# A graph layer on one core: in-place exponentials in two halves, and a third pair buffer in PSUM

## The reference, cut to what matters

```
w_m = (efeat @ W_msg + b_msg).reshape(E, in_f, -1)
w_a = (efeat @ W_attn + b_attn).reshape(E, in_f, -1)
h_src = feat[src][:, :, None]
e1 = w_m * h_src
e2 = w_a * h_src
ex = jnp.exp(e2 - seg_max[dst])
denom = jax.ops.segment_sum(ex, dst, num_segments=N)
ft = jax.ops.segment_sum(e1 * (ex / denom[dst]), dst, num_segments=N)   # then .sum(axis=1)
```

## Time and profile before

| | |
|---|---|
| time, median of 3 runs | 3181.63 us (3181.13 to 3204.2) |
| the profiled execution | 3216.98 us, span 3215.1 us |
| PE busy | 2134.1 us (66%) |
| DVE busy | 1858.7 us (58%) |
| ACT busy | 1255.2 us (39%) |
| POOL busy | 1686.0 us (52%) |
| TensorE clock granted, mean | 0.83 |

### The profile page before, as it was taken

One profiled execution on the slowest core, in us unless ns is written; L12 is line 12 of the kernel. 1 busy time (PEld: TensorE's weight loads), 2 busy tenths in 40 slices (PEclk: granted clock), 3 DMA queues, 4 the chain that ended last, 5 costly groups with the idle time before them and its releaser, 6 DMA issues. The chain is left out here.

```text
span 3215.1 us, 21756 instructions
## 1 busy us (share of the span) xinstructions
PE 2134.1 (66%) x6682; PEld 953.8 (30%) x6682; DVE 1858.7 (58%) x2902; ACT 1255.2 (39%) x1228; POOL 1686.0 (52%) x1845
## 2 busy tenths in 40 slices
PE   2336678667787566766565558687777786667487
PEld 1212233223333222322222223233333332223233
DVE  6235466556665545655454456465667665666386
ACT  3113344334443334433333335353435444343354
POOL 6666555555564554444454444556565664536614
PEclk8657888878898787888887779888899998878799
DMA  6100000000000000000000000000000001001000
GB/s 210 15 14 10 11 10 10 10 9 9 9 14 9 9 9 8 8 12 8 8 9 7 8 7 12 9 9 11 8 12 11 9 12 22 11 7 16 8 1 3
DMA packets 60073, 47.60 MB, mean 15 GB/s; under 512 B 28366, under 2 KB 55439, under 8 KB 59436
## 3 DMA queue, kind: packets, MB, share of 16 engines
q0 software_dynamic: 57632, 29.73, 7.2%
q1 hardware_dynamic: 2316, 16.38, 1.4%
HBM read 44.00 MB, written 1.90 MB: 14 GB/s over the span
## 5 line engine op out<-in xcount | busy, mean ns | idle before, releaser
L652 POOL DMA_INDIRECT AR<-in_xt,AR x1607 | 1538.7, 958 | 751.3 <-issue 494.1
L1128 PE MATMUL PX<-AR,CS 128*128 128x512 f32 x3246 | 1660.3, 640 | 13.5 <-ACT AR L894 8.5
L1472 DVE CUSTOM_DVE_ANT_1 AR<-PW,AR 128x1024 f32<-128x1024 f32 x815 | 978.6, 1221 | 1172.2 <-remote 924.1
L1108 PE MATMUL PW<-WS,LT 100*128 100x512 bf16 x1630 | 551.7, 425 | 976.2 <-DVE AR L1472 755.0
L1128 PEld LDWEIGHTS PX<-AR,CS 128*128 128x128 f32 x3246 | 668.9, 207 | 633.6 <-issue 516.3
L888 ACT ACTIVATE LT<-PTB 100x1024 bf16<-100x1024 bf16 (+1 forms) x221 | 211.3, 956 | 1437.3 <-remote 1017.1
L1485 DVE TENSOR_TENSOR AR<-AR,PX 128x1024 f32<-128x1024 f32 (+1 forms) x442 | 501.2, 1134 | 113.8 <-ACT PX L944 87.1
L1108 PEld LDWEIGHTS PW<-WS,LT 100*128 100x128 bf16 x1630 | 140.0, 102 | 1398.0 <-DVE AR L1472 811.6
L946 ACT ACTIVATE AR<-AR 128x2048 f32<-128x2048 f32 (+1 forms) x221 | 413.0, 1869 | 7.2
L950 ACT ACTIVATE PX<-AR 128x1024 f32<-128x1024 f32 (+1 forms) x221 | 212.3, 961 | 330.7 <-DVE AR L1485 263.0
L657 POOL DMA_INDIRECT AR<-in_es,E0I x48 | 45.4, 946 | 556.2 <-issue 271.9
(11 more groups left out here) (192 smaller groups left out, 517.8 us busy)
## 6 DMA issues: line engine op xcount, KB each, us to landing
AR<-in_xt,AR POOLq DMA_INDIRECT x1607
AR<-in_eat SPq DMA_DIRECT2D x3, 3128.0 KB
AR<-in_eat SPq DMA_DIRECT2D x1, 3120.0 KB
y_d<-AR SPq DMA_DIRECT2D x1, 784.0 KB
AR<-y_d SPq DMA_DIRECT2D x1, 784.0 KB
AR<-in_es,E0I POOLq DMA_INDIRECT x48
y_d<-AR POOLq DMA_INDIRECT x36
CS<-in_cst SPq DMA_DIRECT2D x1, 442.0 KB, 5.3
```

The lines of the kernel that those rows point to most:

```text
L652: g.indirect_dma_start(feat(h, j - j0, j - j0 + 1), None, xt, bass.IndirectOffsetOnAxis(ap=node, axis=0)).then_inc(hg_sem(h), 16)
L1108: i = pe.matmul(PAIRS[s % 2][:, j, :], LT[:, g % 3, lo:lo + 128], WS[:, :], start=True, stop=True)
L1128: i = pe.matmul(PDR, IDN, x, start=(a == 0 and j == 0), stop=(g == LAST[k] and j == n - 1))
L1472: v.tensor_tensor_reduce(em(g, j, j + 2).rearrange("p (x c) -> p x c", c=32), w, hb, 1.0, LOW, ALU.mult, ALU.max, accum_out=MXC[:, k % 2, ...
```

## The change

The two PSUM banks `EXP` become a third pair buffer. Pair s now uses buffer s % 3 and waits for `v_mult` of pair s-3, and PE's W run three pairs ahead instead of two. ACT does two exponentials per group, each of one half and in place; the copy and the waits for `v_gm` are gone. `gm` reads both the messages and the exponentials from SBUF.

```diff
-        PAIRS = [PW[:, 0:2, :], PW[:, 2:4, :]]
-        EXP = PX[:, 0:2, :].rearrange("p b e -> p (b e)")
+        PAIRS = [PW[:, 0:2, :], PW[:, 2:4, :], PX[:, 0:2, :]]
...
                         x, w, shift = weights(c)
                         a.wait_ge(S["v_M"], GRP[c][0] + 1)
-                        if c >= 1:
-                            a.wait_ge(S["v_gm"], 2 * c)
-                        a.activation(half(w), x[:, 0:w, :], ACT.Exp, bias=shift).then_inc(S["a_x"], 1)
-                        a.wait_ge(S["a_x"], 2 * c + 1)
-                        a.activation(x, x, ACT.Exp, bias=shift).then_inc(S["a_exp"], 1)
-                    if c is not None:
-                        a.wait_ge(S["a_exp"], c + 1)
-                        a.wait_ge(S["v_gm"], 2 * c + 1)
-                        a.activation(half(w), x[:, w:2 * w, :], ACT.Copy).then_inc(S["a_x"], 1)
+                        for y in range(2):
+                            z = x[:, w * y:w * y + w, :]
+                            a.activation(z, z, ACT.Exp, bias=shift).then_inc(S["a_x"], 1)
...
-                    if s >= 2:
-                        pe.wait_ge(S["v_mult"], s - 1)
+                    if s >= 3:
+                        pe.wait_ge(S["v_mult"], s - 2)
...
-                        i = pe.matmul(PAIRS[s % 2][:, j, :], LT[:, g % 3, lo:lo + 128], WS[:, :], start=True, stop=True)
+                        i = pe.matmul(PAIRS[s % 3][:, j, :], LT[:, g % 3, lo:lo + 128], WS[:, :], start=True, stop=True)
...
-                            pe.wait_ge(S["a_exp"], g + 1)
+                            pe.wait_ge(S["a_x"], 2 * g + 2)
...
+                W(0, 2)
...
-                    ahead = [(p, x) for x in range(2, GRP[p][2] // 2)] if p is not None else []
-                    ahead += [(nx, 0), (nx, 1)] if nx is not None else []
+                    ahead = [(p, x) for x in range(3, GRP[p][2] // 2)] if p is not None else []
+                    ahead += [(nx, 0), (nx, 1), (nx, 2)] if nx is not None else []
...
-                    w = PAIRS[s % 2].rearrange("p j (i c) -> p (j i) c", c=32)
+                    w = PAIRS[s % 3].rearrange("p j (i c) -> p (j i) c", c=32)
...
-                    y = em(g).rearrange("p (x a o) -> p x a o", a=2, o=16)[:, w * h:w * h + w, 1, :]
-                    v.tensor_tensor(y, y, EXP[:, 0:16 * w].rearrange("p (x o) -> p x o", o=16), ALU.mult).then_inc(S["v_gm"], 1)
+                    y = em(g).rearrange("p (x a o) -> p x a o", a=2, o=16)[:, w * h:w * h + w, :, :]
+                    v.tensor_tensor(y[:, :, 1, :], y[:, :, 1, :], y[:, :, 0, :], ALU.mult).then_inc(S["v_gm"], 1)
```

More of the change, by code:

```diff
@@ L902, in weights @@
                     return em(g).rearrange("p (x a o) -> p x a o", a=2, o=16)[:, :, 0, :], 8 * n, CM[:, 1, k:k + 1]
-                def half(w):
-                    return EXP[:, 0:16 * w].rearrange("p (x o) -> p x o", o=16)
                 def first(k):
@@ L1489, in pairs @@
                     keep = KEPT(half)
-                    v.wait_ge(S["a_exp"], g + 1)
+                    v.wait_ge(S["a_x"], 2 * g + 2)
                     v.wait_ge(S["v_gm"], 2 * g + 2)
```

## The result

The changed kernel took 2890.86 us in the median of four runs (2833.12 to 2950.91), the kernel before 3183.88 us (3181.13 to 3204.2): a ratio of 0.8936, 95% interval 0.883 to 0.9041. The ratio goes by the two shortest runs of the changed kernel. The prediction, 3128 us in a range from 3050 to 3260, had the sign right and missed the time by 237 us, outside its range.

The account below looks back on a forecast made before the run. No one engine bound it: a bin's period was POOL's run of gathers, some 4 us, and a stretch with PE and DVE nearly full. -125 + 75 - 3 = -53 us on 3181.6 gave 3128 us, range 3050 to 3260.

Parts of the forecast that it names:

- the slow stretch: Within POOL's run of gathers in each bin: PE, DVE and ACT nearly stop, 40.5 and 21.7 us, PE's completions arriving late.
- gathers that follow each other less closely let PE's completions through sooner: Rival for the slow stretch: 2 us x 48 gained on top of the forecast, 3032 us; better outcomes together had 0.10.
- The cost on POOL: Weights multiply with two SBUF inputs lengthens gathers in POOL's long runs: 0.45 us on each of 168, +75 us.
- My own rival: POOL's gather runs lengthen more than the buffer saves: 0.8 us per multiply, 134 us, time 3256 us; chance 0.20.
- The gain in PE and DVE: Third pair buffer lets PE and DVE use idle time and adds lead: 2.6 us per bin, -125 us.
- The credit for one more pair at each slow stretch: With a third buffer PE does one more W and two `gsum` slots before it stops: 2.15 us per bin.
- ACT's relief: Two in-place half exponentials take about 2.0 us per large group off ACT; worth nothing on its own.
- the multiply keeps its duration: DVE's weights multiply with both inputs in SBUF: 1.23 us against 1.22 at 1024 columns, counted zero.
- My stop sign: The forecast is wrong if busy time of POOL's gathers, L652, grows by over 150 us.
- The harder form of the rival: DVE's multiply also waits for a gather to end: 0.36 us on average, 60 us more, 3316 us; chance 0.04.

Follow-up runs that it names:

- late case: First comparison, unedited kernels: before 3183.88 us, changed 2890.86 us; many of PE's semaphore increments come late, up to 53 us after the last recorded end.
- prompt case: Every run since, on six chips, PE's increments within 0.02 us: unedited kernel before 2242 to 2246 us, changed kernel 2510.68 us, ratio 1.1203.
- the operand and its wait: Kernel before with the weights multiply's second input taken from SBUF instead of PSUM, and the wait for in-place exponentials: 2484.02 us, ratio 1.1073.
- the 16 of the wait: Kernel before with only the added wait for the in-place exponentials, operand still in PSUM: 2260.58 us, ratio 1.0073.
- POOL relieved: Every second gather of bins 2 to 47 left out, timing only: kernel before 2160.06 us, changed 2140.13 us, changed with two pair buffers 2160.78 us.

## Why the prediction was wrong

**The step that failed is the first one, the slow stretch: "I don't know the mechanism; I take it as the trace shows it."** From there on it stood as a constant of the kernel, POOL's runs plus 4 us. It was neither of the kernel nor constant. The same program without it takes 2242 us, 942 less; since no edit is between the two, it belongs to the chip or to its condition at that time, which the record can't tell apart. And in the late case itself the changed kernel escaped it for hundreds of us at a time: DVE's idle time before its multiplies fell by 301 us, the time by 293. Nor does every run of gathers without a pause bring it on, as I had taken it: in the stretches of 220 and 328 us POOL issues one after the other, each of them longer (1158 and 1166 ns in the mean against 947), and PE's increments are prompt. I had the rival "gathers that follow each other less closely let PE's completions through sooner" and gave it, with another, 0.10 and 3032 us. Its arithmetic, 2 us a bin, allowed a shorter slow stretch and not one that doesn't begin.

Is that rival the cause? It fits: in the late case the gathers did get longer (1061 ns in the mean, more in the good stretches). But it is argued, not shown, and these numbers can't tell cause from effect: where completions are prompt the multiplies run, and where multiplies run the gathers are long. No experiment met the late case, and neither the third buffer nor ACT's part was excluded there. The cause of the 293 us stays open. What the runs do show is that where completions are prompt the three parts together cost 269 us, and that where POOL has room the third buffer alone gives anything, 20 us. So the gain came through the late completions, by whichever part.

**The cost on POOL was mis-sized: +75 forecast, +241 measured in the prompt case for the operand and its wait, 225 without the 16 of the wait.** The direction and the place were right, two numbers were not. The price was 0.45 us per multiply; over all 442 of them it is (1770.8 - 1534.7) / 442 = 0.53. The 0.26 that the 0.45 was raised from came out of the 17 us of excess averaged over 213 short operations. By the trace of before only 60 gathers start inside these operations, so each that does takes some 0.25 us longer, and three in ten of the operations see one start. The long multiply nearly always does: 399 gathers start inside the 442 of the changed kernel and take 0.65 us longer each, 261 us, against the 254 by which the line grew. The count was 168, since in the late case only multiplies inside POOL's runs were to lengthen a bin; where POOL never pauses it is all 442. The count was short in the late case too: there 280 gathers start inside a multiply, and the line grew by 167 us. My own rival put 0.8 us on each of the 168, a price further off than mine; its 134 us, the bound that I gave, was still short because of the count.

**The gain in PE and DVE was mis-sized: -125 forecast, -20 measured** with POOL relieved (2160 to 2140), all by the third buffer. PE is busy 90% there with either. Where the rest of its idle time lies I haven't read, so why a third buffer gives 20 us and not 125 stays open. The credit for one more pair at each slow stretch exists only in the late case and was not measured.

**Right:** ACT's relief is worth nothing by itself (2160.78 against 2160.06 us); the multiply keeps its duration; ACT busy 846 of the forecast 850 us; the median gather still 944 ns; a longer gather, not a slower DVE. The sign of the first comparison was right by luck: where the terms could be measured, the one that carried it gives 20 us, and the cost set against it is 225. My stop sign, "wrong if L652's busy time grows by over 150 us", went off at 167, but with the sign of the time turned round. The harder form of the rival, DVE waiting for gathers, did not come: a multiply that starts inside a gather takes 1221 ns, any other 1223, and in the prompt case L1476's idle time is 124 us, all for ACT's exponentials.

No version with all of its gathers beats the kernel before in the prompt case, and none is known to beat the changed one in the late case.

## What to carry to other kernels

A wait that the profile can't put down to any recorded instruction is first a question about the chip: run the unedited kernel on another one before a model of its bins is built on it. Where POOL issues gathers without a pause, look at every DVE instruction with both inputs in SBUF. Here each weights' multiply of 1.14 us in the mean cost POOL 0.53, so a copy into PSUM by an idle ACT can be worth keeping, however useless it looks in the shares of busy time. A deeper buffer in front of an engine that isn't the bound can cost time, as the 33 us here, because it changes what runs beside what. And average an interference over the moments at which it can happen (a gather's start), not over all instructions.

## What the runs showed of the hardware that I had not expected

The same program, with the same durations on POOL, DVE and ACT, took 3184 us in the first comparison and 2242 to 2246 on six chips since; the difference is in when PE's completions reach the other engines. A gather that starts inside a multiply that reads PSUM loses nothing. In the kernel before, prompt case, the gather at 1233.17 us starts with 0.90 us of the multiply left and takes its usual time:

```profile
1232.85 1.22 DVE L1485 TENSOR_TENSOR AR<-AR,PX 128x1024 f32<-128x1024 f32 x1
1233.17 0.94 POOL L652 DMA_INDIRECT AR<-in_xt,AR  x1 [0.30 <-issue]
```

What makes completions late stays open. It is not a matter of 2400 more small transfers in the prompt case. In both traces of the late case it stands where POOL issues gathers in a row, but not everywhere there.
